# Indirect transfers in eight-wide groups: each group goes out once the whole group in front of it has landed, not the one 9 to 16 back

## What is computed

```
h = max(layernorm(x), 0);  x = x + GAT(h, src, dst)            # two attention layers, 3 heads and 1 head
h = max(layernorm(x), 0);  x = x + RGCN(h, src, dst, type_8)   # two relational layers, 8 relations
h = max(layernorm(x), 0);  x = x + message(h, src, dst, w)     # msg = w*h[src]*h[dst]/(D + E*h[src] + H*h[dst]), summed by src
h = max(layernorm(x), 0);  x = x + edge_matrix(h, attr, src, dst, type_90)
```

## Time and profile before

| | |
|---|---|
| median of three runs | 8142.98 us (8128.08 to 8156.91) |
| time of the profiled execution | 8118.42 us |
| its span in the trace | 8116.7 us |
| PE busy | 3216.4 us (40%), 13056 matmuls |
| DVE busy | 3665.3 us (45%) |
| ACT busy | 1172.6 us (14%) |
| POOL busy | 4283.6 us (53%) |
| DMA | 350.11 MB, mean 43 GB/s |

### The profile page before, as it was taken

How to read it: one execution, slowest core, us unless ns; L and a number is a source line. 1 busy time by engine, 2 the same in 40 slices (tenths; PEclk the granted TensorE clock), 3 DMA queues, 4 the chain that set the end, 5 groups by cost and what they waited for, 6 DMA issues and landing times. The chain is left out here.

```text
span 8116.7 us, 44786 instructions
## 1 busy us (share of the span) xinstructions
PE 3216.4 (40%) x13056; PEld 2477.3 (31%) x13056; DVE 3665.3 (45%) x8916; ACT 1172.6 (14%) x1912; POOL 4283.6 (53%) x3949
## 2 busy tenths in 40 slices
PE   5799999921154105520077312541111100111232
PEld 3688755521043104410066312431111100110221
DVE  8634499840166216750034213784433217411364
ACT  0344455410032003300011000110000000000000
POOL 5544355557600675057700475217888881677565
PEclk9755699955566555555556556665555555555676
DMA  1111122211000212111022111122222223210011
GB/s 35 32 44 47 50 67 66 57 31 10 9 14 12 61 22 64 60 24 15 14 89 92 55 22 33 57 74 38 53 36 38 26 7 127 81 19 16 31 44 52
DMA packets 283354, 350.11 MB, mean 43 GB/s; under 512 B 133518, under 2 KB 204432, under 8 KB 281970
## 3 DMA queue, kind: packets, MB, share of 16 engines
q1 hardware_dynamic: 112158, 295.24, 10.9%
q0 software_dynamic: 169376, 41.40, 6.3%
q10 hardware_dynamic: 1576, 10.60, 0.5%
HBM read 231.06 MB, written 122.29 MB: 44 GB/s over the span
## 5 line engine op out<-in xcount | busy, mean ns | idle before, releaser
L2107 POOL DMA_INDIRECT r_ring<-t_rel,idx x392 | 387.4, 988 | 720.2 <-POOLq L118 506.1
L1466 POOL DMA_INDIRECT g_ring<-t_gat,idx x392 | 398.5, 1017 | 640.0 <-POOLq L118 461.1
L2331 POOL DMA_INDIRECT acc<-l_rows,l_uniq x392 | 627.2, 1600 | 120.4 <-issue 110.6
L502 POOL DMA_INDIRECT pay<-in_x,gidx x392 | 457.7, 1168 | 366.8 <-DVE a_act_t L603 255.5
L2317 POOL DMA_INDIRECT l_ring<-t_mix,idx x392 | 423.2, 1080 | 403.6 <-POOLq L118 284.5
L1796 POOL DMA_INDIRECT r_ring<-t_rel,idx x392 | 398.6, 1017 | 403.2 <-POOLq L118 279.0
L2593 PE MATMUL ps_l<-w_rel,l_pick 128*128 128x256 f32 x784 | 254.3, 495 | 835.3 <-DVE l_pick L2622 494.1
L2552 POOL DMA_INDIRECT l_ring<-t_last,idx x392 | 397.7, 1014 | 330.1 <-ACTq L2547 207.1
L789 POOL DMA_INDIRECT t_sort<-pay,c_pos x392 | 386.1, 985 | 343.2 <-DVE c_pos L855 241.7
L2372 PE MATMUL ps_l<-l_msg,l_alike 128*128 128x16 f32 x784 | 176.1, 375 | 961.5 <-DVE l_msg L2435 928.7
L881 PE MATMUL ps_c<-plane,c_hit 128*128 128x400 f32 x1568 | 544.2, 500 | 1.9 <-ACT c_hit L807 1.9
(11 more groups left out here) (528 smaller groups left out, 8257.3 us busy)
## 6 DMA issues: line engine op xcount, KB each, us to landing
c_rows_d<-row_dst SPq DMA_DIRECT2D x98, 256.0 KB
l_keys<-row_at SPq DMA_DIRECT2D x49, 512.0 KB
l_typs<-row_typ SPq DMA_DIRECT2D x49, 512.0 KB
g_hs<-t_gat SPq DMA_DIRECT2D x30, 660.0 KB
acc<-r_zero SPq DMA_DIRECT2D x60, 320.0 KB
t_rel<-r_row SPq DMA_DIRECT2D x30, 640.0 KB
r_hs<-t_rel SPq DMA_DIRECT2D x30, 640.0 KB
d_gain<-acc SPq DMA_DIRECT2D x30, 640.0 KB
```

The source lines that it names most:

```text
L502: pool.indirect_dma_start(pay[:, s, 8:PAY], None, x, bass.IndirectOffsetOnAxis(gidx[:, s:s + 1], 0)).then_inc(gat_in[s // BATCH], 16)
L1466: pool.indirect_dma_start(ring[:, s % (NR * QN), :], None, t_gat2, bass.IndirectOffsetOnAxis(idx2[:, s:s + 1], 0)).then_inc(gat_in[s // BA ...
L2107: pool.indirect_dma_start(ring[:, s % (NR * QN), :], None, t_rel2, bass.IndirectOffsetOnAxis(idx2[:, s:s + 1], 0)).then_inc(gat_in[s // BA ...
L2331: pool.indirect_dma_start(acc[r], bass.IndirectOffsetOnAxis(uniq[:, s:s + 1], 0), rows[:, (s // ES) % RR, s % ES, :], None, compute_op=ALU.add
```

## The change

`paced` waits for the group directly in front instead of the one before that, and it does so only at a group's first transfer:

```diff
 def paced(engine, landing, s, first=0):
-    n = s // BATCH - 2
-    if n >= first // BATCH:
+    n = s // BATCH - 1
+    if s % BATCH == 0 and n >= first // BATCH:
         engine.wait_ge(landing[n], 16 * BATCH)
```

## The result

| | before | after |
|---|---|---|
| time, median of 3 runs (us) | 8142.98 (8128.08 to 8156.91) | 7019.89 (7000.82 to 7023.58) |
| ratio | | 0.8615, 95% interval 0.858 to 0.8649 |
| profiled execution, span | 8116.7 | 7021.8 |
| PE, DVE, POOL busy | 40%, 45%, 53% | 46%, 52%, 61% |

The forecast was 6980. What it did not foresee came with the experiments: the kernel before does not take the same time on every chip. On three of the five chips used for them it takes 8099 to 8164 us, as above; on the other two 6496 to 6552. On one of these two both kernels ran several times, and there the change costs 6.7%.

What follows compares the result with a forecast made beforehand. PE crawls while POOL issues gathers each 1.25 us to something serving one per 1.40 us. Savings 325 + 185 + 385 + 205 - 10 + 60 = 1150 us gave 6968 to 6993, forecast 6980, range 6760 to 7700.

Steps and rivals of the forecast that it cites:

- The crawl: Passes A to D: PE starts one instruction per 1.40 us while POOL streams gathers without a break; gone with chance 0.75.
- The rival that PE needs an idle POOL: Passes A to D and F: a 1.4 us gap is too short, the crawl stays, 8310 us; chance 0.13.
- lifted in part: At a group nearer 10.9 us the backlog returns after 15 to 20 groups; half the gain, 7560 us; chance 0.09.
- the 28.1 us of the earlier trace: Pass F: a DVE step waiting for PE comes 28.1 us late, at 7720.18; 40 scatters at 1.402 from 7666 give 7722.
- The gap per group: POOL's new wait for a group's last landing: 1.4 us for gathers, ends 1.2 and 2.84; group 11.4 us.
- C and D: Streamed passes: C saves 385 us, D 205, with 49 groups of 11.4 us, 559 us of stream each.
- the work behind the streams: Work left after a pass's gathers: some 65 us in C, 121 us of matmuls in D.
- A and B: Streamed passes: A saves 325 us, B 185; some 110 and about 100 us of work stand behind their streams.
- F: Last pass: 60 us saved; gathers 49 x 11.3 = 554 us, scatters 11.1 a group, 545 us.
- The 118 us of waits for DVE: Pass F: the 118.4 us in which POOL waits for DVE go, as a freed DVE needs less.
- Up to A: Stretch before pass A's first transfer: predicted saving 0.
- The sum: Savings of A, B, C, D and F less 10 in L2317's pass: 1150 us.

Runs made afterwards that it cites:

- slowing without a landing wait: 192-column memset on POOL ahead of each paced transfer, pacing of before, no landing wait, against the kernel before: 6987.43 us, ratio 0.8606 on the first chip.
- a shorter memset: Memset of 16 columns instead of 192 ahead of each paced transfer, pacing of the kernel before: 7833.68 us on the first chip (one run).
- the every-second-group kernel: The changed kernel's wait for the group directly in front, only at every second group, against the kernel before: 7810.84 us, ratio 0.9605 on the first chip.
- half rows: Kernel before with pass C's gathers fetching 64 of 128 rows: 6554.27 us beside 6501.84 (second chip), 8144.66 beside 8099.11 (fourth).

## Why the prediction was right, and which terms were off

**The mechanism.** The crawl beside an unbroken stream, and its end by issuing more slowly, are shown: by slowing without a landing wait, and by a shorter memset that takes off 4% alone. The rival that PE needs an idle POOL is refuted. That the crawl is lifted in part is refuted for the changed kernel (PE is free to the end of each stream), and is what the every-second-group kernel does.

Two things in the account were wrong, though the forecast didn't hang on them. PE isn't fed instructions one by one; its counts reach the other engines late. And what queues isn't transfers that wait to be carried out. At one served per 1.402 us, the starts of POOL in pass C of the kernel before give a backlog of 19 by the 233rd transfer, and POOL goes at 1.400 from there on (17 in pass A, and 17 x 1.40 = 24 us is about what the crawl outlives that stream by). The pacing lets at most fifteen be under way, yet no wait for a landing is seen. The last landing that the trace holds of each of that pass's 49 groups is at most 1.51 us behind the end of its last transfer on POOL, and the copy behind the last scatter came after 1.21 us. So something goes at 1.40 us a transfer and at 1.40 us a PE instruction, and the rows moved are not in its queue. The agreement of the 28.1 us of the earlier trace rows with 40 scatters at 1.402 may be chance: 28.0 is also 20 PE instructions.

**The gap per group** was mis-sized: 1.4 us predicted. The medians over the groups after are 1.70 in A, 1.74 in B, 1.66 in C, 2.84 in D, 1.65 and 1.41 in F; the means 1.77, 2.17, 1.92, 2.57, 1.84 and 1.51. Why D's are longer stays open; they are so on the third chip too (2.82). I took the nearest row to be the last scatter's 1.21 to SP's copy; the row for that in the changed kernel is about the same,
```profile
6992.69 0.96 POOL L2563 DMA_INDIRECT fin<-X,home_i  x1 [0.30 <-issue]
6995.53 0.96 POOL L2563 DMA_INDIRECT fin<-X,home_i  x1 [1.89 <-DMA fin<-X,home_i]
6997.71 0.60 SPq L2578 DMA_DIRECT2D out<-fin  x1
```
with 1.22 us from the end of the last scatter (6996.49) to the copy, but POOL's own wait for a whole group, in the line above the copy's, is 1.89, and a gather's 1.7: the row of one engine's wait for one transfer was no measure of another's for eight. With the transfers 1.05 us long instead of 1.02 the group was 12.6 us in A to D, not 11.4. That is 49 x 1.2 = 59 us more in a full pass (50 in A with its 42 groups, 48 in B, for which I had 11.7). The savings of A, B and C fell short by 55, 26 and 5, and D's was 30 more than forecast. The Trainium skill, "DMA: Bandwidth & Descriptors", section "Anatomy of one DMA — SWDGE (gpsimd) path", gives about 2 us for the set-up and completion of one such DMA. Read as the gap, as the prediction did, that was nearer than my row for the gathers, whose mean gaps of 1.77 to 2.57 us stand on both sides of it; the scatters' 1.51 was nearer to my row.

**C and D** came out at 380 and 235 against 385 and 205 in spite of the longer group, so the work behind the streams was over-counted there: 33 us (3660 to 3693) in C, where I had put 65, and 36 in D, where I had put 121 us of matmuls; and from C's saving I had taken 19 us off for work beside the stream, which the longer group used up.

**A and B** have about the work behind the stream that I read from the order (109 and 77 us against 110 and 100).

**F** saved 17 instead of 60. The gathers took 588.7 us (12.0 a group, not 11.3), and the scatters 580.1 to the end. The 118 us of waits for DVE went as foreseen.

**Up to A** I counted nothing, and 45.5 went. 26.7 of it is the block of 56 gathers of L964 (116.0 to 89.3), the same crawl in small: 1.03 matmuls a microsecond there before, 1.86 after. I had not looked for the crawl outside the large passes. The other 19 lie in the first pass, whose length differs that much between executions with no change in it (776 to 898 us over the profiled runs here).

**The sum** came within 40 us of the median, closer than its terms: A, B and F fell short by 124 us in all, and the 45.5 us up to A and D's 30, neither of them foreseen, made up for most of it. That is luck.

**What the prediction could not have from one trace** is the condition. It wrote the 1.40 us down as the server's own; it was seen on three of the five chips alone. That the change was timed where the kernel before crawls was no merit of the forecast. With the sizes of the chips without it, pass A 586.0 us, B 627.9, D 553.2, F 506.5 and 521.4, against the changed kernel's stages above, the change costs 52, 69, 98, 82 and 59 us, with C's some 57 (592 us with half rows) and 12 in L2317's pass: 429, against 415 measured between the medians.

## What to carry to other kernels

When engines that have little to do with a stream of indirect transfers do next to nothing beside it (here 247 PE instructions in 345 us, in bursts), look at how long after PE's last matmul the engine that needs its count starts. Where that is tens of us, try a slower stream: a cap on how many transfers are under way can be worth more than the time it adds. Compare how many semaphore counts the traces hold, too. Run both kernels on several chips before keeping such a cap, since here it saved 14% on one and cost 7% on another. A delay tuned to a rate is fragile: in the traced execution on one chip it freed a pass that it left 200 us longer on the next.

## What was not expected of the hardware

- The crawl went with the chip, in 23 runs of the kernel before over five chips, each used at one time. The wait for a landing is the same on both kinds (median 1.70 us in pass A of the changed kernel on the chip with the crawl, 1.69 on the third), so a group that starts with none under way lands no later. What makes PE's counts late stays open.
- It doesn't go by rows: 64 and 128 crawl alike, and POOL's mean time for one is the same in pass C: 1016 ns with half the rows on the fourth chip, 1017 with all before.
- The edge is narrow and the state lasts: a natural period of 1.39 us frees every pass in the traced execution on one chip and all but one on another, a mean of 1.36 to 1.38 leaves A and C crawling, and in pass D of the fifth chip the crawl persisted at a mean of 1.42.
- POOL is itself held in it: from the 215th gather of pass A and the 233rd of pass C on, the kernel before goes at a mean of 1.400 us, where it started at 1.25.
- Not tried: a cap that slides, transfer by transfer (at most so many not yet landed). It might pause less than the wait for a whole group on either kind of chip. Nor was any kernel timed with the recording known to be off.
